# A selective-scan block on eight cores: scan inputs kept as bf16 in DRAM, and the step-size work of ScalarE put back into its own chunk

## The reference, cut to what matters

```python
xz = x @ in_proj_w.T
x_ssm, z = split(xz)                       # 2048 channels each
xc = silu(causal_conv4(x_ssm))
xp = xc @ x_proj_w.T                       # 33 numbers per token
dt_r, Bv, Cv = xp[..., :1], xp[..., 1:17], xp[..., 17:]
dt = softplus(dt_r @ dt_proj_w.T + dt_proj_b)
dA = exp(dt[..., None] * A)                # 16 states per channel
dBx = dt[..., None] * Bv[:, :, None, :] * xc[..., None]
h_t = dA_t * h_{t-1} + dBx_t               # scan over 2048 tokens
y_t = sum_n h_t[n] * C_t[n]
y = y + xc * D
out = (y * silu(z)) @ out_proj_w.T
x = x + layernorm(out)
```

## Time and profile before

| | us |
|---|---|
| median of 2 runs | 8117.14 |
| lowest, highest | 8101.81, 8132.48 |
| the profiled execution | 8126.19 |
| its span on the slowest core (core 5) | 8124.4 |
| spans of the other cores | 8084.0 to 8116.4 |

### The profile page before, as it was taken

How to read it: one execution, slowest core, us unless ns; L and a number is a source line. 1 busy time by engine, 2 the same in 40 slices (tenths; PEclk the granted TensorE clock), 3 DMA queues, 4 the chain that set the end, 5 groups by cost and what they waited for, 6 DMA issues and landing times.

```text
span 8124.4 us, 45481 instructions; the slowest of 8 cores (8084.0 to 8124.4 us)
## 1 busy us (share of the span) xinstructions
PE 2954.5 (36%) x11136; PEld 1126.4 (14%) x11136; DVE 3912.5 (48%) x5725; ACT 1959.2 (24%) x2902; POOL 338.0 (4%) x639
## 2 busy tenths in 40 slices
PE   6200011000200012000631777777776646647272
PEld 3000000000000000000210222222222212223131
DVE  6189935998189944999130222222222343331414
ACT  4132212332132312222211333333331000021212
POOL 0100010000100010000100000000000000000000
PEclk9655556555655555555765777777777767768696
DMA  2500043000700033000386111111111111111211
GB/s 65 46 7 0 0 34 56 0 0 7 74 9 0 0 34 56 0 0 1 88 97 83 21 17 21 21 21 21 21 16 40 50 43 57 52 54 62 73 63 48
DMA packets 112654, 275.76 MB, mean 34 GB/s; under 512 B 19144, under 2 KB 39624, under 8 KB 111116
## 3 DMA queue, kind: packets, MB, share of 16 engines
q0 software_dynamic: 69200, 178.17, 16.3%
q1 hardware_dynamic: 33980, 77.91, 3.1%
q10 hardware_dynamic: 9216, 16.78, 0.6%
HBM read 339.04 MB, written 63.51 MB: 50 GB/s over the span
## 4 chain that ended last, share of the span: by engine, by line
DVE 34%; PE 29%; issue 11%; another core or an unknown queue 10%; ACT 8%; DMA 6%; SPq 1%; DVEq 1%; ACTq 0%; POOL 0%; POOLq 0%
DVE h_band L725 16%; PE psF L1310 6%; PE psF L1529 6%; PE psF L1337 5%; ACT attT L1349 4%; DVE h_band L737 4%; PE psF L1728 3%; PE psF L1740 3%; PE psF L1324 2%; PE psF L918 2%; DVE h_band L746 2%; DVE xc_a L1581 2%; DMA wzD<-winp_z 1%; PE psF L1510 1%
## 5 line engine op out<-in xcount | busy, mean ns | idle before, releaser
L725 DVE TENSOR_TENSOR_SCAN h_band<-daD,hcol,dxD 128x512 f16<-128x512 f32 x1024 | 1303.1, 1278 | 162.0 <-ACT daD L629 159.7
L629 ACT ACTIVATE daD<-dtD,c_A 128x512 f32<-128x512 f32 x1024 | 732.3, 721 | 1826.6 <-DVE h_band L725 1816.9
L593 PE MATMUL psA<-woD,xc_a 128*128 128x512 bf16 x256 | 79.6, 442 | 2740.8 <-DVE xc_a L775 2721.1
L1349 ACT ACTIVATE attT<-psF 128x1024 bf16<-128x1024 f32 x512 | 498.0, 1022 | 641.3 <-PE psF L1324 635.7
L1398 DVE TENSOR_TENSOR ost<-psF,rlbG 64x512 bf16<-64x512 f32 x64 | 42.4, 680 | 1134.4 <-DMA rlbG<-lrow 528.8
L1310 PE MATMUL psF<-wvG,act_a 128*128 128x512 bf16 x2048 | 500.6, 402 | 174.7 <-DVE ost L1398 147.1
L1529 PE MATMUL psF<-xc_a 128*128 128x512 bf16 x2048 | 475.8, 397 | 30.7 <-DVE xc_a L1581 30.7
L1324 PE MATMUL psF<-qT_aug,kT_aug 65*128 65x512 bf16 x1024 | 386.0, 484 | 205.2 <-ACT attT L1349 202.8
L720 DVE TENSOR_TENSOR dxD<-uD,bb_sb 128x512 bf16<-128x512 bf16 x960 | 408.0, 425 | 95.6 <-DVE h_band L725 2.8
L1337 PE MATMUL psF<-attT,v_aug 128*65 128x512 bf16 x1024 | 381.7, 554 | 88.4 <-ACT attT L1349 88.4
L593 PEld LDWEIGHTS psA<-woD,xc_a 128*128 128x128 bf16 x256 | 23.7, 105 | 2793.7 <-issue 2790.6
(11 more groups left out here) (219 smaller groups left out, 3646.2 us busy)
## 6 DMA issues: line engine op xcount, KB each, us to landing
xc_a<-wob POOLq DMA_DIRECT2D x128, 256.0 KB, 4.6
wzD<-winp_z POOLq DMA_DIRECT2D x64, 256.0 KB, 4.1
woD<-woutT POOLq DMA_DIRECT2D x64, 256.0 KB, 4.9
wob<-wo POOLq DMA_DIRECT2D x1, 16384.0 KB, 305.9
wvG<-wv POOLq DMA_DIRECT2D x32, 512.0 KB, 6.1
xc_a<-w1b POOLq DMA_DIRECT2D x64, 256.0 KB, 6.5
xc_a<-w2b ACTq DMA_DIRECT2D x64, 256.0 KB, 7.6
xreD<-xin SPq DMA_DIRECT2D x16, 512.0 KB, 4.3
```

Of the source, the lines that this page charges most:

```text
L629: inc(s.activation(daD[n % 2][:], dt[:], AF.Exp, scale=c_A[:, dc * NN + n: dc * NN + n + 1]), "da")
L725: last = v.tensor_tensor_scan(h_band[:, n * TW:(n + 1) * TW], daD[n % 2][:], dxD[n % 2][:], hcol[:, dc * NN + n: dc * NN + n + 1], op0=OP. ...
L1349: inc(s.activation(attT[:, (2 * grp) * 512:(2 * grp + 2) * 512], psF1[:, slot:slot + 1024], AF.Exp, scale=0.125), "gs")
```

## The change

1. `xp_d` becomes bf16, and so do the two staging tiles `xpstg`. The stores to `xp_d` and the 32 loads of B and C rows are then plain copies from bf16 to bf16, with pieces of 1 KB; the load of `dtr_b` now casts from bf16 to float32. `dt_r` is rounded to bf16 on this way; B and C were rounded to bf16 before too.
2. ACT's program no longer computes dt of the next chunk's block 0 ahead of the epilogue. It does so in its own chunk, after the 16 Silus. The counts of the semaphores `dts`, `scv` and `da` that others wait for stay as they are. POOL's, SP's, PE's and DVE's programs are unchanged.

```diff
-    d_xpd = nc.dram_tensor("xp_d", [65, S], F32, kind="Internal").ap()
+    d_xpd = nc.dram_tensor("xp_d", [65, S], BF16, kind="Internal").ap()
...
-    xpstg = [sbb(f"xpstg{i}", [128, 512], F32) for i in range(2)]
+    xpstg = [sbb(f"xpstg{i}", [128, 512], BF16) for i in range(2)]
...
-            def dt_only(ttc, dc):
-                gidx = ttc * DC + dc
+            for dc in range(DC):
+                gidx = tc * DC + dc
                 if dc == 0:
-                    wge(s, "gb", QG_TCB[ttc])
+                    wge(s, "gb", QG_TCB[tc])
                 dt = dtD[dc % 2]
                 if gidx >= 2:
                     wge(s, "scv", (gidx - 1) * NN)
@@
                 last = s.activation(dt[:], dt[:], AF.Ln, bias=1.0)
                 wge(s, "dts", inc(last, "dts"))
-
-            def da_loop(ttc, dc):
-                dt = dtD[dc % 2]
                 for n in range(NN):
-                    gn = gni(ttc, dc, n)
+                    gn = gni(tc, dc, n)
                     if gn >= 3:
                         wge(s, "scv", gn - 2)
                     inc(s.activation(daD[n % 2][:], dt[:], AF.Exp,
                                      scale=c_A[:, dc * NN + n: dc * NN + n + 1]), "da")
-            if tc > 0:
-                da_loop(tc, 0)
-            for dc in range(0 if tc == 0 else 1, DC):
-                dt_only(tc, dc)
-                da_loop(tc, dc)
-            if tc + 1 < TC:
-                dt_only(tc + 1, 0)
```

## The result

The changed kernel takes 7908.9 us (median of 11 runs, 7857.2 to 8026.3); the kernel before took 8129.1 us beside it. The ratio is 0.9721, with an interval of 0.9687 to 0.9754: about 226 us less on 8117. The forecast was 94 us less. The direction is right and the size is not; 7909 lies in the range, and by its figure next to the rival "in between" (7923), 98 us above "by bytes" (7811). One of the 11 runs (8026.3) fell, like some runs of the other kernels, into a slower state with a lower granted clock on one die; the ratios here leave such runs out, and so do the times of e12, e13 and e14, beside which only two runs of the kernel before are left, hence their wide intervals.

What follows compares the result with a forecast made beforehand. `gb` transfers, epilogue and Silus stood in series at chunk boundaries. The order change saves 106 us less 12 for traffic, bf16 nothing: 8117 - 94 = 8023 us; own range 8000 to 8065, 8-in-10 range 7790 to 8065.

Steps and rivals of the forecast that it cites:

- in between: Rival for the `gb` loads: part fixed cost per read, part by bytes; saving 25 us a stretch, time 7923; chance 0.13.
- by bytes: Rival for the `gb` loads: each takes half, 53 us saved per stretch, 306 us in all, time 7811; chance 0.25.
- I take 107, by the layernorm rows.: `gb` transfers: 33 loads still take 107 us in bf16, because 4 KB layernorm pieces were read at 283 GB/s.
- I take 4 per boundary: Chunk boundaries: epilogue traffic beside the `gb` transfers costs 4 us each, 12 in all, nearer the lower bound of 0.
- The upper bound of 16: Chunk boundaries: 5.2 MB of epilogue traffic at 320 GB/s costs 16 us if it adds to the transfers in full.
- takes what it takes after the last chunk: Epilogue at the first boundary: 37.6 us beside the transfers, ending near 1178, 67 us before the z weights land.
- PE idle about 107 us under a z weight: Sign at PE: it waits about 107 us for z weights queued behind `gb` loads as long as before.
- First scan 58 us after the first z matmul: Sign at each boundary: 58.3 us from first z matmul to first scan, with Silus and dt, as in chunk 0.
- `wzD` landing at 96, 43 or 20 us: Sign at the z weights, time from issue: about 96 says by packets, about 43 by bytes, under 20 fast.
- A DMA rate over 60 GB/s in the epilogue: Sign in the epilogue: with `wzD` landing above 112 us, it would say the traffic adds and the forecast is wrong.
- The traffic adds in full: Rival at the boundaries: the epilogue's traffic adds wholly to the `gb` transfers, time 8059; within the case given 0.50.
- The rival with fast loads: Rival for the `gb` loads: as fast as other loads, 22 us instead of 107, time 7723; chance 0.07.

Runs made afterwards that it cites:

- e12: Changed kernel with rows of the bf16 `xp_d` padded so they lie 5 KB apart instead of 4 KB; ratio 0.956, 7739.2 us.
- e13: e9 with its rows put 4 KB apart again, 3 KB of each left unused; ratio 0.9669, 7833.5 us.
- e14: e9 in float32, with ACT's new order: 2 KB pieces lying 2 KB apart, chunk by chunk; ratio 0.9633, 7804.1 us.
- e2: Kernel before with only `xp_d` and its staging in bf16, ACT's old order kept; ratio 0.9717, 7916.6 us.
- e8: e3 with the 16 Silus of a chunk moved from ahead of its scans into each one's own block; ratio 0.9256, 7534.8 us.
- e9: Changed kernel with `xp_d` laid out chunk by chunk, rows 1 KB apart instead of 4 KB, still 32 loads of 1 KB pieces; ratio 0.9571, 7737.4 us.
- e10: e9 with 2 rows per load: 16 loads of 2 KB pieces per chunk; ratio 0.9556, 7736.2 us.
- e6: Changed kernel with `xp_d` laid out chunk by chunk and 4 rows per load: 8 loads of 4 KB pieces; ratio 0.9513, 7743.6 us.
- e3: Changed kernel with `xp_d` laid out chunk by chunk, 16 rows per load: pieces of 16 KB, 3 loads per chunk instead of 33; ratio 0.9541, 7768.6 us.
- e5: e1 with every partition reading its own 2 KB row of a float32 weight matrix instead of one shared piece; 7734.6 us, one run.
- e1: Kernel before with only ACT's order changed, `xp_d` and `xpstg` left in float32; ratio 0.9961, 31 us less.
- e7: e1 without the 15 reloads of x in the epilogues, so its output is wrong; ratio 0.9892, 8060.7 us.

## Why the prediction was right or wrong

**The reading of before held.** The `gb` transfers, the epilogue and the Silus did stand in series. Shorten the first (e2) and the scan part shrinks by just that (211 us, four times 53); take the Silus out (e8) and the first scan comes right behind the epilogue.

**Part 1, the failed step: "I take 107, by the layernorm rows."** The loads took half as long, not as long: ACT's wait shrank by 53.3 us at each boundary (e2), which leaves 53.7 of the 107, and four times 53 are the 212 us that this step put at nothing. The step set 80 GB/s for a 2 KB piece beside 283 GB/s for a 4 KB piece and took the difference for an effect of size. Those two differ in more than size, and the size is nearly without effect (e9, e10, e6, e3). The 283 GB/s wasn't pure either: loads of `o_sp` run in the same stretch, in packets of 2 KB, and the two layernorm rows, 512 KB each, landed 4.6 and 6.0 us after their issue. The steps ahead of it were right, and each is confirmed: not the cast (e5 and e14 cast too), not the engines (e3: the same engines bring the same bytes in 19 us), but the source. Behind "so it is the source" I asked only for bytes or packets, and didn't ask what about the source was slow. That a source held at a fixed rate would go by bytes followed from the list itself, and should have had more than 0.25. That it did come out at half fits this, but the distance of the rows halved with the bytes, so what sets the slow rate stays open between the two. A premise was wrong too: the number of packets did not stay (last section), so a fixed time a packet could not have given 107 us.

**Part 2, the mis-sized term: "I take 4 per boundary".** The upper bound of 16 was the truth: 17.7 us at the first boundary and 14.9 and 16.2 at the others (e1), 10.6 for three fifths of the traffic (e7). The argument for the lower end, a low rate at a share of 0.54, didn't carry: what comes beside transfers held at their source still adds to them in full. The Trainium skill's rule that was set against it (DMA: Bandwidth & Descriptors, Issuing engines are not separate DMA queues) is what e1 shows. The epilogue "takes what it takes after the last chunk", 37.6 us, failed as well: its own reloads are slowed by the `gb` transfers. In e1 most took 26 to 30 us from issue to landing; in the changed kernel the first two of the boundary took 37.5 and 19.7. In float32 the epilogue still ends before the z weights, and that costs nothing. In bf16 it ends after them.

**The sum, mended.** The 306 us of the rival "by bytes" had 12 us taken off for the traffic; without that it is 318. By its figures the first scan would come 118.9, 120.7 and 116.9 us after the issue of `dtr_b` at the three boundaries. The cores of the changed kernel show 143.9, 140.8 and 137.1 in the mean, 65 us more in all. Of the 25 us at the first, 10 are z weights that come later (70.3 against 60.2), and 15 the epilogue that outlasts them (73.6 from there to the first scan, against 58.3). 318 - 65 = 253, where the scan part shrank by 245.8 and the times by 226. Most of the last 7 us is the core that was profiled: before, its three boundaries took 9 us more than the cores' mean.

**Point by point of what would show it.** ACT's wait for `cb_sb` gone: yes. ACT's first pass right behind DVE's first sum: yes, 1088.22 behind 1086.90. First Silu right behind the first z matmuls: no, 18.4 us late. PE idle about 107 us under a z weight: 63.2. dt behind the last Silu: yes, at 1218.41. First scan 58 us after the first z matmul: 71.6. `wzD` landing at 96, 43 or 20 us: 56.2, by bytes plus traffic. A DMA rate over 60 GB/s in the epilogue: 106 GB/s from 1100 to 1130 us.

**The rivals.** "By bytes" was the mechanism, and its time too low by what the traffic costs. "The traffic adds in full" was true at the same time. I had weighed the two as alternatives, and they came together. The rival with fast loads (7723) is what e9 and e12 reach (7737, 7739) once the distance is mended.

## What to carry to other kernels

If many small loads, each read by all partitions, are slow and neither their engines nor their cast explain it, look at the distance in DRAM from row to row before anything else: a padded row is one number in the source, and on top of the bf16 it took another 122 us off the scan part (3635.4 to 3513.6). When work is moved beside a transfer to hide there, count the DMAs of the moved work twice: they stretch the transfer, and they are themselves late. And a comparison of two rates is one of sizes only if nothing else differs; the control that changes one thing is cheap, and e9 overturned a theory that two runs (e3, e6) had seemed to support.

## What the runs showed of the hardware that was not expected

- 128 readers of one 1 KB piece, 33 loads in a row, ahead of chunk 0 of the changed kernel: with rows 4 KB apart 52.5 us from the first landing to the last, 80 GB/s. With 5 KB or 1 KB a load lands 7.5 to 8.4 us after its issue (median at the first boundary), and the first 20 keep up with POOL's 0.53 us a load.
- Loads held up by their source at 80 GB/s read (40 written in float32) leave nothing over for others: a reload of 512 KB, 4.3 us in the median of the kernel before, took 13.2 in the median of a boundary of the changed kernel and 37.5 at most, and traffic beside the float32 loads lengthens them at about 300 GB/s.
- Without the cast the packets are other ones. The page of before counts 112654 packets, 39624 of them under 2 KB; that of the changed kernel 100622 and 23500. So 16124 small ones are gone, nearly all of the 16384 (4 x 32 x 128) of B and C, and 4092 larger ones stand in their place, four pieces to a packet. The time went to half, as the bytes read and the distance of the rows did, and not to a quarter as the packets.
